# Q, K and V projections in three half-precision products of split operands, in a differential-attention and mixture-of-experts kernel

## The reference

```python
Q = (x @ Wq).reshape(B, S, NUM_HEADS, 2 * HEAD_DIM).transpose(0, 2, 1, 3)
K = (x @ Wk).reshape(B, S, NUM_HEADS, 2 * HEAD_DIM).transpose(0, 2, 1, 3)
V = (x @ Wv).reshape(B, S, NUM_HEADS, HEAD_DIM).transpose(0, 2, 1, 3)
...
attn = jax.nn.softmax(A1, axis=-1) - lamb * jax.nn.softmax(A2, axis=-1)
```

## Time and profile before

| what | value |
|---|---|
| median of three runs | 3121.12 us (3114.9 to 3121.22) |
| the profiled execution, its own time | 3120.4 us |
| its span in the trace | 3118.7 us |
| projection stage, first item on TensorE | 15.96 us |
| projection stage, last V product begins | 172.43 us |
| first work of the attention stage on TensorE | 176.97 us |

### The profile page before, as it was taken

One profiled execution on the slowest core, in us unless ns is written; L12 is line 12 of the kernel. 1 busy time (PEld: TensorE's weight loads), 2 busy tenths in 40 slices (PEclk: granted clock), 3 DMA queues, 4 the chain that ended last, 5 costly groups with the idle time before them and its releaser, 6 DMA issues. The chain is left out here.

```text
span 3118.7 us, 77478 instructions
## 1 busy us (share of the span) xinstructions
PE 2974.4 (95%) x30985; PEld 1279.1 (41%) x30986; DVE 2857.7 (92%) x3113; ACT 2585.2 (83%) x4760; POOL 624.5 (20%) x696
## 2 busy tenths in 40 slices
PE   8999999999999999999999999999999997799995
PEld 4433333333333333333333333333333356699994
DVE  3589999999999999999999999999999948788886
ACT  2259999999999999999999999999999964566664
POOL 2011101110110011011101110110011036465565
PEclk9989999999999999999999999999999998799997
DMA  6631202110211112021202110211110145332224
GB/s 156 130 57 52 36 9 49 36 36 9 49 46 29 29 49 36 16 36 44 44 9 49 36 36 9 49 41 33 30 49 15 69 162 209 114 49 48 48 47 135
DMA packets 111752, 170.10 MB, mean 55 GB/s; under 512 B 24056, under 2 KB 70896, under 8 KB 108752
## 3 DMA queue, kind: packets, MB, share of 16 engines
q1 hardware_dynamic: 97808, 146.81, 18.8%
q0 software_dynamic: 13632, 18.91, 3.8%
HBM read 97.00 MB, written 68.68 MB: 53 GB/s over the span
## 5 line engine op out<-in xcount | busy, mean ns | idle before, releaser
L1054 DVE TENSOR_REDUCE half_max<-scores 128x2 f32<-128x1024 f32 x2016 | 2295.9, 1213 | 10.4 <-PE scores L807 4.6
L978 ACT ACTIVATE probs<-bank 128x512 f32<-128x512 f32 x4012 | 2141.6, 594 | 142.8 <-PE bank L820 45.2
L879 PE MATMUL bank<-probs,V 128*32 128x256 f32 x16384 | 1310.5, 392 | 44.2 <-ACT probs L978 42.3
L807 PE MATMUL scores<-K,Q 48*128 48x512 f16 x4032 | 793.8, 388 | 2.7 <-SPq L550 2.2
L820 PE MATMUL bank<-Q,K 50*128 50x512 f16 x4012 | 790.1, 380 | 0.0
L879 PEld LDWEIGHTS bank<-probs,V 128*32 128x32 f32 x16384 | 322.7, 108 | 582.6 <-issue 516.8
L807 PEld LDWEIGHTS scores<-K,Q 48*128 48x128 f16 x4032 | 194.2, 93 | 834.0 <-DVE half_max L1054 531.5
L820 PEld LDWEIGHTS bank<-Q,K 50*128 50x128 f16 x4012 | 371.3, 94 | 184.2 <-ACT probs L978 4.2
L686 POOL TENSOR_SCALAR max_parts<-row_max 128x16 f16<-128x16 f32 x64 | 16.3, 254 | 1910.0 <-DVE row_max L1060 1910.0
L1618 PE MATMUL pre<-xs,w 128*128 128x128 f16 x3408 | 205.1, 221 | 3.9 <-DVE xs L1727 3.9
L1637 PE MATMUL py<-W,hs 128*128 x1704 | 199.1, 274 | 3.5 <-DVE hs L1731 3.0
(11 more groups left out here) (202 smaller groups left out, 1467.4 us busy)
## 6 DMA issues: line engine op xcount, KB each, us to landing
w_in<-in_L_ffn_w_dram SPq DMA_DIRECT2D x32, 512.0 KB, 4.8
attended<-att SPq DMA_DIRECT2D x64, 256.0 KB, 3.0
Q<-q_parts SPq DMA_DIRECT2D x96, 128.0 KB, 6.3
K<-k_parts SPq DMA_DIRECT2D x96, 128.0 KB, 7.0
values<-attended SPq DMA_DIRECT2D x6, 2048.0 KB, 10.6
q_parts<-parts SPq DMA_DIRECT2D x64, 128.0 KB, 2.4
k_parts<-parts SPq DMA_DIRECT2D x64, 128.0 KB, 2.4
w_parts<-w_out SPq DMA_DIRECT2D x16, 512.0 KB, 5.4
```

The source lines that it names most:

```text
L807: mm = nc.tensor.matmul(scores[:, b, h, :], Q[p][r, c, up, t * P:(t + 1) * P], K[p][r, up, kc * TC:(kc + 1) * TC], start=True, stop=True)
L879: mm = nc.tensor.matmul(banks[att_bank[s // KB]][32 * u:32 * u + 32, q], V[wp][:, wk, u // 2, :], probs[:, 4 * s % RING + u, q], start=(wk ...
L978: nc.scalar.activation(probs[:, i % RING, :], banks[tile_bank[i]][:], ACT.Exp, scale=SCALE).then_inc(exp_done, 1)
L1054: nc.vector.tensor_reduce(half_max[lc % 2][:, :, up, t, kc], scores[:, b], AX.X, ALU.max).then_inc(max_done[b], 1)
```

## The change

Each operand of the three projections is cut into two half-precision parts, a high part (the value rounded) and a low part (the rest rounded). A product is then three half-precision products: high x high, high x low, low x high (`PRODUCTS`).

- x: ScalarE multiplies `xT` in place by 16 and writes the high part into `x_cut` (`high_x`); GpSimd subtracts and writes the low part (`low_x`). For chunks 0 and 1 this is done ahead of everything; for a later chunk ScalarE does its two operations in the chunk before, ahead of item 4 (`HIGH_AT`).
- Wv: ScalarE scales and rounds, GpSimd subtracts.
- Wq and Wk: VectorE writes the high parts as before (now half precision) and then sixteen low parts, first all of Wq, then all of Wk.
- TensorE's waits for a loaded x become waits for `x_low`; the load of a later x waits for `x_low` in place of `v_ready`.
- The scale of the products is taken out in the operations that read PSUM: ScalarE's copies become multiplications by a constant, and VectorE's low part becomes one operation with a factor.

```diff
-        wqk = sb("wqk", [P, KD, 2, 2 * D], F32)
+        wqk = sb("wqk", [P, 2, KD, 2, 2 * D], F16)
+        wvs = sb("wvs", [P, 2, KD, D], F16)
+        x_cut = [sb(f"x_cut{i}", [P, 2, KD, TC], F16) for i in range(2)]
...
+        PRODUCTS = ((0, 0), (0, 1), (1, 0))
...
                     if i == COLS_AT and 1 <= n < NC - 1:
-                        sp.wait_ge(v_ready, 2 * n)
+                        sp.wait_ge(x_low, n)
                         load_cols(n + 1)
...
+            def low_x(n):
+                pool.wait_ge(x_high, n + 1)
+                nc.gpsimd.tensor_tensor(x_cut[n % 2][:, 1], xT[n % 2][:], x_cut[n % 2][:, 0], ALU.subtract).then_inc(x_low, 1)
...
-            pool.wait_ge(wqk_ready, 4 * KD)
+            low_x(0)
+            pool.wait_ge(wv_high, 2)
+            nc.gpsimd.tensor_tensor(wvs[:, 1], wv[:], wvs[:, 0], ALU.subtract).then_inc(wv_low, 1)
+            low_x(1)
...
+            for n in range(2, NC):
+                low_x(n)
...
+            def high_x(n):
+                act.wait_ge(cols_loaded[n % 2], 16 * (n // 2 + 1))
+                if n >= 2:
+                    act.wait_ge(v_ready, 2 * (n - 1))
+                    act.wait_ge(proj_ready, ITEMS * (n - 1))
+                    act.wait_ge(x_low, n - 1)
+                nc.scalar.mul(xT[n % 2][:], xT[n % 2][:], 2.0 ** LIFT_PX).then_inc(x_lifted, 1)
+                act.wait_ge(x_lifted, n + 1)
+                nc.scalar.copy(x_cut[n % 2][:, 0], xT[n % 2][:]).then_inc(x_high, 1)
...
+            act.wait_ge(wv_loaded, 16)
+            nc.scalar.mul(wv[:], wv[:], 2.0 ** LIFT_PV).then_inc(wv_high, 1)
+            act.wait_ge(wv_high, 1)
+            nc.scalar.copy(wvs[:, 0], wv[:]).then_inc(wv_high, 1)
+            high_x(0)
+            high_x(1)
             copy_values(0)
             for n in range(NC):
                 for i in range(ITEMS):
+                    if i == HIGH_AT and 1 <= n < NC - 1:
+                        high_x(n + 1)
                     act.wait_ge(proj_ready, n * ITEMS + i + 1)
...
-                    nc.scalar.copy(parts[:, i % 4, 0, :], pj[i % 4][:]).then_inc(hi_ready, 1)
+                    nc.scalar.mul(parts[:, i % 4, 0, :], pj[i % 4][:], UNLIFT).then_inc(hi_ready, 1)
...
-                        mm = nc.tensor.matmul(pv[j // 2][:, j % 2, :], xT[n % 2][:, k, j * P:(j + 1) * P], wv[:, k, :],
-                                              start=(k == 0), stop=(k == KD - 1), skip_group_check=True)
+                        for at, (xp, wp) in enumerate(PRODUCTS):
+                            mm = nc.tensor.matmul(pv[j // 2][:, j % 2, :], x_cut[n % 2][:, xp, k, j * P:(j + 1) * P],
+                                                  wvs[:, wp, k, :], start=(k == 0 and at == 0),
+                                                  stop=(k == KD - 1 and at == 2), skip_group_check=True)
...
-            pe.wait_ge(wv_loaded, 16)
-            pe.wait_ge(cols_loaded[0], 16)
+            pe.wait_ge(x_low, 1)
+            pe.wait_ge(wv_low, 1)
             times_wv(0, range(1))
...
-                pe.wait_ge(cols_loaded[n % 2], 16 * (n // 2 + 1))
+                pe.wait_ge(x_low, n + 1)
                 for i in range(ITEMS):
+                    if n == 0 and i % MC == 0:
+                        pe.wait_ge(wqk_ready, 4 * KD * (i // MC + 1))
...
-                        mm = nc.tensor.matmul(pj[i % 4][:], wqk[:, k, i // MC, (i % MC) * P:(i % MC + 1) * P],
-                                              xT[n % 2][:, k, :], start=(k == 0), stop=(k == KD - 1))
+                        for at, (wp, xp) in enumerate(PRODUCTS):
+                            mm = nc.tensor.matmul(pj[i % 4][:], wqk[:, wp, k, i // MC, (i % MC) * P:(i % MC + 1) * P],
+                                                  x_cut[n % 2][:, xp, k, :], start=(k == 0 and at == 0),
+                                                  stop=(k == KD - 1 and at == 2))
...
+            for m in range(2):
+                for k in range(KD):
                     for h in range(2):
+                        nc.vector.tensor_scalar(split(wqk[:, 0, k, m, :])[:, h], joint(wraw[:, k, m, :])[:, h],
+                                                lift[:, m:m + 1], None, ALU.mult).then_inc(wqk_high, 1)
+                for k in range(KD):
+                    for h in range(2):
+                        dve.wait_ge(wqk_high, 2 * KD * m + 2 * k + h + 1)
+                        for u in range(2):
+                            nc.vector.scalar_tensor_tensor(split(wqk[:, 1, k, m, :])[:, h, :, :, u],
...
-                nc.vector.tensor_tensor(parts[:, i % 4, 1, :], pj[i % 4][:], parts[:, i % 4, 0, :],
-                                        ALU.subtract).then_inc(lo_ready, 1)
+                nc.vector.scalar_tensor_tensor(parts[:, i % 4, 1, :], pj[i % 4][:], UNLIFT, parts[:, i % 4, 0, :],
+                                               ALU.mult, ALU.subtract).then_inc(lo_ready, 1)
```

More of the change, by code:

```diff
@@ L40 @@
 LIFT_X = 3
+LIFT_PX = 4
+LIFT_PW = 4
+LIFT_PV = 7
 ONE = 2.0 ** 15
@@ L132, in stage_project @@
     COLS_AT = 2
+    HIGH_AT = 4
     half_max, PRE, KC, KB = (a[n] for n in ("half_max", "PRE", "KC", "KB"))
@@ L156, in stage_project @@
                  "w_peaked", "peaks_turned", "lift_chain", "lift_bits_ready", "lift_spread", "lift_ready",
-                 "ones_set", "group_loaded")
+                 "ones_set", "group_loaded", "wqk_high", "x_lifted", "x_high", "x_low", "wv_high", "wv_low")
         (wqk_loaded, wv_loaded, ident_ready, wqk_ready,
          proj_ready, hi_ready, lo_ready, v_ready, values_ready, w_peaked, peaks_turned, lift_chain,
-         lift_bits_ready, lift_spread, lift_ready, ones_set, group_loaded) = (sem(n) for n in names)
+         lift_bits_ready, lift_spread, lift_ready, ones_set, group_loaded, wqk_high, x_lifted, x_high, x_low, wv_high, wv_low) = (
+             sem(n) for n in names)
+        PRODUCTS = ((0, 0), (0, 1), (1, 0))
+        UNLIFT = 2.0 ** -(LIFT_PX + LIFT_PW)
         parts_stored = [sem(f"parts_stored{i}") for i in range(4)]
@@ L250, in _ @@
             pool.wait_ge(ident_ready, 3)
-            pool.wait_ge(wqk_ready, 4 * KD)
+            low_x(0)
+            pool.wait_ge(wv_high, 2)
+            nc.gpsimd.tensor_tensor(wvs[:, 1], wv[:], wvs[:, 0], ALU.subtract).then_inc(wv_low, 1)
+            low_x(1)
+            pool.wait_ge(wv_low, 1)
+            pool.wait_ge(x_low, 2)
             for i in range(2):
@@ L269, in copy_values @@
                     act.wait_ge(v_ready, 2 * n + j // 2 + 1)
-                    nc.scalar.copy(values[:, b * G:(b + 1) * G, c * TPC + j, :],
-                                   pv[j // 2][:, j % 2, :].rearrange("p (g f) -> p g f", g=G)
-                                   ).then_inc(values_ready, 1)
+                    nc.scalar.mul(values[:, b * G:(b + 1) * G, c * TPC + j, :],
+                                  pv[j // 2][:, j % 2, :].rearrange("p (g f) -> p g f", g=G),
+                                  2.0 ** -(LIFT_PX + LIFT_PV)).then_inc(values_ready, 1)
+            def high_x(n):
[13 more added lines that the diff above has]
+            high_x(1)
             copy_values(0)
@@ L323, in _ @@
             times_wv(0, range(1, TPC))
-            pe.wait_ge(wqk_ready, 4 * KD)
             for n in range(NC):
-                pe.wait_ge(cols_loaded[n % 2], 16 * (n // 2 + 1))
+                pe.wait_ge(x_low, n + 1)
                 for i in range(ITEMS):
+                    if n == 0 and i % MC == 0:
+                        pe.wait_ge(wqk_ready, 4 * KD * (i // MC + 1))
                     if n * ITEMS + i >= 4:
@@ L356, in _ @@
             dve.wait_ge(lift_chain, 4)
-            nc.vector.tensor_scalar(lifted[:], lean[:], float(127 + LIFT), None, ALU.add).then_inc(lift_chain, 1)
+            nc.vector.tensor_scalar(lifted[:], lean[:], float(127 + LIFT + LIFT_PW), None, ALU.add).then_inc(lift_chain, 1)
             dve.wait_ge(lift_chain, 5)
@@ L363, in _, with split, joint @@
             dve.wait_ge(lift_ready, 1)
-            for k in range(KD):
-                for m in range(2):
-                    for h in range(2):
[L367 to L370, removed]
+            def split(v):
+                return v.rearrange("p (g h d u) -> p h g d u", h=2, d=HD, u=2)
+            def joint(v):
+                return v.rearrange("p (g u h d) -> p h g d u", h=2, d=HD, u=2)
+            for m in range(2):
+                for k in range(KD):
+                    for h in range(2):
+                        nc.vector.tensor_scalar(split(wqk[:, 0, k, m, :])[:, h], joint(wraw[:, k, m, :])[:, h],
[5 more added lines that the diff above has]
+                            nc.vector.scalar_tensor_tensor(split(wqk[:, 1, k, m, :])[:, h, :, :, u],
+                                                           joint(wraw[:, k, m, :])[:, h, :, :, u], lift[:, m:m + 1],
+                                                           split(wqk[:, 0, k, m, :])[:, h, :, :, u],
```

(8 more changed lines are left out.)

## The result

The changed kernel is slower: its six runs have a median of 3133.84 us (3128.27 to 3137.48), the six of before 3119.15 us (3114.9 to 3121.22); the ratio is 1.0049, 95% interval [1.0039, 1.0059]. The forecast was 3112.7 us, and its range ended at 3121. The profiled execution took 3128.98 us, 8.6 more than the profiled one of before. It is the second quickest of the six, so the trace shows 8.6 of the 14.7 us between the medians; the four longer runs have a lower granted clock (0.972 to 0.974 for its 0.975), and no trace shows where.

A forecast was written before the change was run, and what follows sets the result against it. TensorE was taken as the bound. A head later by 4.6 us and the chunks' changes ended the stage at 166.3 where it was 174.74: -8.4 us against the median of 3121.1, 3112.7 us; range 3106 to 3121.

The forecast's parts named there:

- the head: Start of the first stage: Wq ready at 20.5 us where the first item began at 15.96, later by 4.6 us.
- Item length: TensorE's products of one projection item: six half-precision ones at 0.215 us, 1.29 us, for 1.716 before.
- Chunk 0: First chunk of the stage: no new wait, eight items in 10.3 us for 13.7.
- Chunks 1 to 3: First-stage chunks held by the split of x: 14.1 us for chunk 1, 15.1 each for chunks 2 and 3.
- the chain of x: x through SyncE's load, ScalarE and GpSimd: sets chunk 1 at 14.1 us, 1.1 over TensorE's own pace.
- a sign of being wrong by the prediction's own list: In chunks 1 to 3: a granted clock under 1.00 would show the forecast wrong.
- Chunk 4: Chunk waiting for the loads of the first attention group: no gain, 26.3 us.
- Chunks 5 and 6: Items with attention pairs: 23.3 us each, with ScalarE's stall for x and one half-clock stretch per chunk.
- Chunk 7: Last chunk of the stage: no x to fetch, 18.3 us, end at 166.3 where it was 174.74.
- the first rival: Chunks' gain eaten by loads landing in 5.8 us, or clock falling in waits between chunks 1 to 4: 3118 to 3121; chance 0.32.
- The second rival: x is hidden: ScalarE's wait costs nothing, chunks 1 to 3 take 12.95 us, time 3097; chance 0.06.
- The slower rival: Half clock stays from a stall in chunk 5 through chunk 7: three chunks 99 us, time about 3147; chance 0.07.

The follow-up runs named there:

- e1: The changed kernel, but GpSimd's constant rows of K wait again until VectorE has made all parts of Wq and Wk; 3119.63 us, ratio 1.0002.
- e4: e1 with the load of the next x asked for two items earlier, ahead of item 0's stores; 3095.73 us, ratio 0.9923 to the kernel before.

## Why the prediction was wrong

**The step that failed is the head.** Its sentence that GpSimd's constant rows "start behind its third subtraction at 17.2 and end before 35" was right to 0.1 us on the start, and it asked only who reads the rows. It did not ask what runs beside them: four operations which the kernel before had kept apart from them by a wait. So it put this overlap at nothing, without a reason. It priced "Four high parts at 2.21 / 8 = 0.28" from a row in which no memset ran; they took 14.32 us, 3.58 each. Wq was forecast ready at 20.5; the first item, which waits for it, began at 34.02, 13.5 us later. The rest of the head held to 0.3 us: the first V tile at 15.27 (15.1), the lift's copy at 17.25 (17.2), eight low parts in 2.18 (2.2).

**The sum by chunks.** The stage was forecast to end at 166.3 and ended at 183.40, 17.1 later: 13.5 in the head, 1.7 in chunk 0, 1.6 in chunk 1, 0.7 and 0.6 in chunks 2 and 3, 0.1 in chunk 4, -0.7, 0.7 and -1.1 in chunks 5 to 7. The median lies 21.1 us above the forecast; the other 4 us are in runs without a trace.

- *Item length*: 48 products in 10.53 us (the last drain in it), right; forecast 10.3.
- *Chunk 0*: the clock came back at half level, 1.2 GHz for 2.4, after the wait (0.50 granted in the first 2 us, 0.85 over the chunk), a cost of the same memsets; in e1, with full clock, 96 products take 20.88 us.
- *Chunks 1 to 3*: the chain of x is there as described: x lands in 4.4 to 4.7 us (4.4 taken), ScalarE waits for it ahead of item 4 in six chunks, 30.4 us in all (3.7 to 4.9 each, 9.3 in chunk 4), TensorE waits for GpSimd's x. Each chunk took 0.6 to 1.6 us more than forecast. Most of it is x asked for later: SyncE was busy with the stores of chunk 0 until 49.81 (one of them took 1.48 us, the others 0.61) and issued the x load 6.5 us after the start of chunk 1, not 5.35; in chunks 2 and 3 it was 6.9 and 6.8. ScalarE came to its wait in chunk 1 after 6.3 us, not 3.4, since four high parts stand ahead of it; that cost nothing. Chunk 2 ran at a granted clock of 0.90, a sign of being wrong by the prediction's own list, yet it is as long as chunk 3 at 1.00 (15.77 and 15.74): in both TensorE waits for x at the end.
- *Chunk 4*: right (26.38). Its wait became longer, 10.84 for 5.93, as much as TensorE got shorter.
- *Chunks 5 and 6*: right to 0.7, with one half-clock stretch in each (0.92 and 0.86 granted).
- *Chunk 7*: 17.23 for 18.3; VectorE's pair is faster than taken (one every 1.72 us, forecast 1.83).

**The rivals.** With the memsets out of the way (e1, 3119.63) the first rival's time comes true, 3118 to 3121, and of its two causes the second, in part: the clock fell in the waits ahead of e1's chunks 3 and 4 (48 products in 12.12 and 12.13 us), while the loads of chunks 1 to 3 took 4.4 to 4.6 us. A third cause stood in no rival: e1's chunk 1 took 16.3 us for 14.1 at full clock, since SyncE, still with the stores of chunk 0, issued the x load only 7.3 us after its start. The forecast itself would have missed by 7 us even without the memsets. The rule on the clock that the prediction took from the Trainium skill, "TensorE: Matmul & The Clock Gate", section "HAM oscillation — how this bites in real kernels", is told there of one other kernel and its waits; taken for every wait it is too strong for these rows: in the kernel after, the wait of 2.44 us was followed by half clock (12.07 us for 48 products), the waits of 1.08 and 2.59 were not (10.53), nor was e1's of 3.17. The second rival's price, 3097 with x hidden, was good: e4 has 3095.73. The slower rival, half clock that stays, did not occur; the kernel was slower by a mechanism that stood in no rival.

## What to carry to other kernels

A wait that a change removes may have kept two engines apart as well as ordered their data: for every instruction that moves, look at what then runs beside it on VectorE and GpSimd, and price that overlap, even where nobody reads the result for a long time. Where one engine gets faster, look whether its input has to be asked for earlier; here two items or two chunks earlier made a change of no gain into one of 0.8%. A duration from a row holds only beside the same neighbours.

## What was not expected of the hardware

- A one-input operation of VectorE on SBUF took 3.5 us in place of 0.35 while a GpSimd memset ran, and ended about 0.15 us after it. It lost to every memset of a row of four, while these took 14.30 us for 14.18: nearly all of the price is VectorE's.
- A two-input operation was not held by a memset (8 in 2.20 us) but was held by a two-input subtraction on GpSimd (2.22 us for 0.35).
- After a wait of 2 to 3 us TensorE sometimes came back at 1.2 GHz and sometimes at 2.4: in e1 the wait of 2.45 us was followed by 12.12 us for 48 products (granted clock 0.50 at their start), a wait of 3.17 us by 10.53 (1.00). What decides it stayed open.
